# A graph network's edge rounds: matmul operands read in place by a register address, and three transfers a round in place of twelve

## The chip, the cores and the metric

One core of a Trainium2 chip runs the whole kernel in one launch. The time is the device time in microseconds (us) of one execution; the median of three is compared. The engines are TensorE (PE), VectorE (DVE), ScalarE (ACT), GpSimd (POOL) and SyncE (SP). Each runs its own instruction stream, and they are held together by semaphores alone.

## What is computed

The inputs are 6,250 nodes with 256 features and 200,000 edges, sorted by destination. Three layers of graph attention run over the edges and the nodes' own loops; beside them runs a linear-attention mixing block, and behind both a mixture of eight experts. Only the edge part of the attention layers bears on this change:

```python
xh = (h @ W).reshape(n, heads, d)
a_s = (xh * att_src).sum(-1)
a_d = (xh * att_dst).sum(-1)
alpha = jax.nn.leaky_relu(a_s[src] + a_d[dst], NEG_SLOPE)
amax = jax.ops.segment_max(alpha, dst, num_segments=n)
e = jnp.exp(alpha - amax[dst])
z = jax.ops.segment_sum(e, dst, num_segments=n)
alpha = e / (z[dst] + 1e-16)
out = jax.ops.segment_sum(xh[src] * alpha[:, :, None], dst, num_segments=n)
```

The kernel spreads `a_d`, the term of the destination node, over the edges, finds each destination's greatest score, and adds up the weighted rows of the source nodes.

## The kernel before

**Blocks, groups and rounds.** Nodes lie in 49 blocks of 128 (`NB`). Edges are cut into groups of 256 (two halves of 128, one edge per partition), and all edges of a group have their destinations in one block. A round, called a window in the code, takes `WG` = 10 groups, so `WS` = 20 halves; a layer has `NW` = 83 rounds, three layers 249. Buffers of a round come in a ring of `RING` = 4. `over_windows` runs each engine's `step` over the rounds in a loop of four, its first and last rounds written out; each engine has its own order of work for several rounds at once.

**What each engine does in the edge phase.**
- POOL gathers the source nodes' rows, one indirect transfer of 128 rows for each half (L1123). It waits for the indices (L1134 on ScalarE) and, four gathers at a time, for the sums of the round four before, whose buffers it takes.
- SyncE loads per round: four copies of the scan masks and eight small rows of links (`load_masks`, L1026 to L1037), and one broadcast of the edges' place in their block (`load_rels`, 640 KB, L1045). In layer 2 it also loads three constants of the mixing block, behind the first four rounds' masks, and in layer 0 it clears a buffer of the experts.
- ScalarE makes the indices, copies ten node tiles (`load_node`, L1137 to L1143), makes the exponentials of the scores (L1150, L1151) and of the fade (L1160). Its order in a step is: index, exponentials, `load_node` for four rounds ahead, fade, mixing.
- TensorE: `spread_ad` multiplies 20 one-hot halves with the node tiles (L1275), 128 x 12 bf16 for each; `turn` and `turn_back` transpose the scores and the greatest scores (L1284, L1292); `spread_fade` (L1304); `sums` adds the weighted rows of ten groups, four float32 passes each (L1317). Its order in a step is: sums of groups 0 to 4, `spread_fade`, `turn`, sums 5 to 8, `spread_ad` for three rounds ahead, sum 9, the mixing's matmuls, `turn_back`.
- VectorE: one-hots of the edges' places (L1444, L1449), the sums of the spread terms (L1455), scores (L1462, L1467), two scans with the masks over the edges for the greatest score (L1476, L1481), small transposes and scans over the lanes, differences (L1543), weighting of the gathered rows (L1563), one-hots (L1555), and ten adds of the sums into the blocks' accumulators (L1581).

**Block numbers in registers.** Which block each group of a round belongs to is packed in one 32-bit word a round. `blocks_of` (L1014 to L1022) loads the word into a register and unpacks ten block numbers, each from the one before by a shift, a mask and an add. ScalarE and VectorE each run it; ScalarE uses it for the addresses of `load_node`.

**Mixing.** In about the first 49 rounds of each layer a node tile of the mixing block is worked on beside the edges: some 30 more instructions a round on ScalarE, VectorE and SyncE together and about 4 us of matmuls on TensorE (L1329 to L1372), in `mixes`. The rounds behind them have edges only.

**Semaphores that the change touches.** `node_ready` counts ScalarE's filled node tiles, `ad_spread` TensorE's finished spreads, `masks_in[n]` the landed transfers of buffer n, 16 for each of twelve; `walk_out` the transfers of the preparation.

Of the kernel before, what the change touches and what calls it, by code (L numbers as in the profile page):

```python
# [15 lines left out]
BF16 = mybir.dt.bfloat16  # L16
I32 = mybir.dt.int32
ALU = mybir.AluOpType
ACT = mybir.ActivationFunctionType
AX = mybir.AxisListType  # L20

P = 128
# [6 lines left out]
H = 4  # L29
# [5 lines left out]
WG = 10  # L35
WS = 2 * WG
# [82 lines left out]
def prepare_walk(nc, src, dst, st, dr):  # L119
# [6 lines left out]
    with Phase(nc, "walk") as ph:  # L126
# [77 lines left out]
        def _(sp):  # L204
# [34 lines left out]
            for c, n in chunks():  # L239
                sp.dma_start(dr["lanes"].rearrange("(g j) x -> g (j x)", j=2)[c * P:c * P + n, :],  # L240
                             lanes[0:n, c, :, :, :].rearrange("p j m e -> p (j m e)")).then_inc(walk_out, 16)
            sp.wait_ge(links_ready, 2)
# [4 lines left out]
            sp.wait_ge(walk_out, 16 * GC * 6)  # L247
# [564 lines left out]
def edge_phase(nc, layer, st, io, dr):  # L812
# [13 lines left out]
    with Phase(nc, f"edges{layer}") as ph:  # L826
        G = [ph.sb(f"G{r}", [P, WS, GW]) for r in range(RING)]
        index = [ph.sb(f"index{r}", [P, WS], I32) for r in range(RING)]
        node = [ph.sb(f"node{r}", [P, WG, KEPT], BF16) for r in range(RING)]
# [43 lines left out]
        node_ready = ph.sem("node_ready")  # L873
# [151 lines left out]
        def _(sp):  # L1025
            def load_masks(i, n):  # L1026
                w = RING * i + n

                if not isinstance(w, int) or w >= RING:
                    wait_apart(sp, greatest_ready, w - RING + 1, passed_sp)  # L1030
                for h in range(H):
                    sp.dma_start(masks[LANES * h:LANES * h + WS, n, 1:1 + 3 * P], dr["lanes"][bass.ds(w * WS, WS), :]
                                 ).then_inc(masks_in[n], 16)
                for h in range(H):
                    for k, row in ((0, LANES * h), (1, LANES * h + LANES - 1)):
                        sp.dma_start(links[row:row + 1, n, :, :], dr["links"][k:k + 1, :, bass.ds(w * WS, WS)]
                                     ).then_inc(masks_in[n], 16)  # L1037
# [91 lines left out]
        def _(a):  # L1129
# [7 lines left out]
            def load_node(i, n):  # L1137
                w = RING * i + n

                wait_past(a, ad_spread, w - RING + 1)  # L1140
                for g, b in enumerate(blocks_of(a, w)):
                    ins = a.activation(node[n][:, g, :], terms[:, bass.ds(b, 1), :, :].rearrange("p a h k -> p (a h k)"), ACT.Copy)  # L1142
                ins.then_inc(node_ready, 1)  # L1143

# [19 lines left out]
            for n in range(RING):  # L1164
                load_node(0, n)

            def step(i, n, mix):
                if mix:
                    centres(i, n)
                if exists(i, n, 1 + RING):  # L1170
                    make_index(*later(i, n, 1 + RING))
                if exists(i, n, 1):
                    exponentials(*later(i, n, 1))
                if exists(i, n) and exists(i, n, RING):
                    load_node(i + 1, n)
                if exists(i, n, 1):
                    fades(*later(i, n, 1))
                if mix:
                    mixes(i, n)
# [86 lines left out]
        def _(pe):  # L1266
            def spread_ad(i, n):
                w = RING * i + n
                pe.wait_ge(oht_ready, 2 * w + 2)
                pe.wait_ge(node_ready, w + 1)  # L1270

                wait_past(pe, ad_ready, w)
                wait_past(pe, ran, w)
                for s in range(WS):
                    mm = pe.matmul(ps_ad[:, s * KEPT:(s + 1) * KEPT], OHT[:, s, :], node[n][:, s // 2, :], start=True, stop=True)  # L1275
                mm.then_inc(ad_spread, 1)
# [136 lines left out]
        def _(v):  # L1413
# [56 lines left out]
            def scan_on(i, n):  # L1470
                w = RING * i + n
                v.wait_ge(turned, w + 1)
                v.wait_ge(masks_in[n], 16 * 3 * H * i + 16 * 3 * H)
# [1091 lines left out]
def build(nc, io, out):  # L2565

    def dram(name, shape, dt=F32):
# [4 lines left out]
          "lanes": dram("lanes", (2 * NG, 3 * P), BF16), "links": dram("links", (2, 2, 2 * NG), BF16),  # L2572
# [63 lines left out]
```

## Time and profile before

| what | value |
|---|---|
| median of 3 runs | 9471.33 us (9468.83 to 9475.12) |
| profiled execution | 9454.66 us, span 9453.0 us |
| mean granted TensorE clock | 0.724 |
| mean DMA rate over the span | 116 GB/s |
| PE, DVE, POOL, ACT busy | 56%, 58%, 55%, 19% |
| edge phases | three, of 2,449, 2,640 and 2,653 us |

The profile is of one execution. Busy time counts the work of an engine, not its register, branch, semaphore and transfer-issuing instructions. "Idle before" is the time in which the engine did no work ahead of an instruction, and the name behind it what ended that: another engine's instruction, a transfer, "remote" for a semaphore whose raiser the profile doesn't name, or "issue" where the engine waited for nothing that the profile shows, which includes its own register instructions.

### The profile page before, as it was taken

To read this page: it belongs to the slowest core of one execution; us is meant where nothing else is said; L and a number is where in the kernel's file an instruction comes from. 1 tells how busy PE (TensorE), PEld (TensorE's weight loads), DVE (VectorE), ACT (ScalarE), POOL (GpSimd) and SP (SyncE) were. 2 spreads that over 40 slices of the span, in tenths; PEclk is the share of its full clock that TensorE was granted. 3 is DMA by queue.
4 is the path that set the end of the run, shared out by engine and by line. 5 is a ranking of instruction groups with operands and counts; after the bars stand their busy time and mean duration, and the time that the engine had idled before them with its cause. 6 is when DMAs were issued, how large, how long until landed. Compare 5 with 4: busy or idle time off the path is not lost. (4 is left out here: it accounts for less than half of the span.)

```text
span 9453.0 us, 126480 instructions
## 1 busy us (share of the span) xinstructions
PE 5285.4 (56%) x21872; PEld 3724.2 (39%) x21873; DVE 5524.3 (58%) x14694; ACT 1795.1 (19%) x6145; POOL 5206.4 (55%) x5539
## 2 busy tenths in 40 slices
PE   4256666655556255565655556266656565553397
PEld 2144444433334144444443334144444443333255
DVE  4355655555558366665665558366666665557543
ACT  2011111110103012222210002122222220102333
POOL 3566666666662565656566662566666666661332
PEclk7677777776667577777776676577777777766699
DMA  3444444444442343444343333344444443334333
GB/s 118 113 137 130 138 130 136 136 129 133 131 132 87 105 117 111 119 113 118 114 117 110 108 112 108 106 114 121 120 120 120 122 116 112 111 107 132 113 55 75
DMA packets 540784, 1098.15 MB, mean 116 GB/s; under 512 B 136232, under 2 KB 332639, under 8 KB 540147
## 3 DMA queue, kind: packets, MB, share of 16 engines
q0 software_dynamic: 274368, 731.65, 28.9%
q1 hardware_dynamic: 264803, 361.17, 12.1%
q14 instruction: 400, 3.28, 0.1%
q8 instruction: 61, 1.00, 0.0%
q10 hardware_dynamic: 1152, 1.05, 0.0%
HBM read 953.54 MB, written 148.64 MB: 117 GB/s over the span
## 5 line engine op out<-in xcount | busy, mean ns | idle before, releaser
L1123 POOL DMA_INDIRECT edges_G<-rows,edges_index x4980 | 4749.2, 954 | 3076.4 <-issue 1389.8
L1317 PE MATMUL edges_ps_o<-edges_G,edges_OH 128*128 128x264 f32 x9960 | 3620.3, 517 | 2818.6 <-DVE acc L1581 1740.4
L1317 PEld LDWEIGHTS edges_ps_o<-edges_G,edges_OH 128*128 128x128 f32 x9960 | 2357.1, 253 | 3772.9 <-DVE acc L1581 1852.1
L1581 DVE TENSOR_TENSOR acc<-acc,edges_ps_o 128x264 f32 x2490 | 1056.9, 424 | 1992.7 <-remote 1038.9
L1563 DVE TENSOR_TENSOR edges_G<-edges_G,edges_ps_c 128x1024 f32<-128x1024 f32 x1245 | 1501.5, 1206 | 44.1 <-ACT edges_G L1151 33.3
L1142 ACT ACTIVATE edges_node<-terms 128x12 bf16 x2490 | 495.9, 210 | 2316.7 <-issue 2283.7
L1555 DVE TENSOR_TENSOR edges_OH<-edges_ps_c,relT 128x512 f32<-128x512 f32 x1245 | 847.1, 681 | 30.5 <-issue 19.2
L1150 ACT ACTIVATE edges_ps_c<-edges_diff 128x80 f32<-128x80 f32 x249 | 60.0, 241 | 2402.8 <-DVE edges_diff L1543 2174.5
L2400 POOL DMA_INDIRECT x<-experts_Y,experts_token x105 | 162.1, 1544 | 373.5 <-issue 211.5
L1476 DVE TENSOR_TENSOR_SCAN edges_run<-edges_masks,edges_ps_s 128x128 f32<-128x128 bf16 x249 | 102.9, 413 | 444.0 <-ACT edges_fade L1160 286.9
L1275 PEld LDWEIGHTS edges_ps_s<-edges_node,edges_OHT 128*128 128x128 bf16 x4980 | 181.5, 104 | 296.6 <-issue 248.8
L1275 PE MATMUL edges_ps_s<-edges_node,edges_OHT 128*128 128x12 bf16 x4980 | 173.3, 172 | 219.9 <-issue 123.7
L1449 DVE TENSOR_SCALAR edges_OHT<-edges_rels,lane 128x1280 bf16<-128x1280 bf16 x498 | 258.8, 561 | 0.0
L2423 PE MATMUL experts_psH<-W,experts_xs 128*128 x420 | 209.6, 622 | 43.5 <-issue 43.3
L1543 DVE TENSOR_TENSOR edges_diff<-edges_alpha,edges_ps_s 128x80 f32<-128x80 f32 x249 | 57.2, 230 | 301.4 <-DMA xn<-node_Hn 106.3
L799 PE MATMUL node_psB<-node_Wx,node_hT 128*128 128x264 f32 x588 | 213.8, 500 | 0.0
L1988 POOL DMA_INDIRECT xslot<-final_XH,final_slots x98 | 97.6, 996 | 198.0 <-DVE final_slots L2168 169.9
L2438 PE MATMUL experts_psY<-W,experts_hT 128*128 x840 | 198.8, 379 | 0.9 <-DVE experts_hT L2527 0.9
L583 POOL DMA_DIRECT2D rows<-node_ext x147 | 80.0, 544 | 212.1 <-ACT node_ext L757 172.3
L2520 DVE TENSOR_TENSOR experts_hid<-experts_psH,b 128x512 f32<-128x512 f32 x105 | 72.6, 691 | 210.9 <-PE experts_psH L2423 202.9
L1444 DVE TENSOR_SCALAR edges_front<-edges_ps_c,edges_rels 128x128 f32<-128x128 f32 x249 | 85.3, 343 | 133.2 <-DMA edges_rels<-rel 60.1
L1304 PEld LDWEIGHTS edges_ps_s<-edges_dropped,edges_front 128*128 128x128 f32 x498 | 119.7, 241 | 108.8 <-issue 80.7
(345 smaller groups left out, 6399.7 us busy)
## 6 DMA issues: line engine op xcount, KB each, us to landing
edges_rels<-rel SPq DMA_DIRECT2D x249, 640.0 KB
edges_G<-rows,edges_index POOLq DMA_INDIRECT x4980
xslot<-edges_blank SPq DMA_DIRECT2D x80, 650.0 KB
edges_links<-links SPq DMA_DIRECT2D x1992, 0.1 KB
rows<-node_ext POOLq DMA_DIRECT2D x147, 130.0 KB, 2.4
edges_masks<-lanes SPq DMA_DIRECT2D x996, 15.0 KB
experts_X<-xslot SPq DMA_DIRECT2D x105, 130.0 KB, 2.1
node_rows<-rows SPq DMA_DIRECT2D x98, 130.0 KB, 2.1
```

The source lines that it names most:

```text
L799: pe.matmul(psB[slot % 2][:, 0:RW + H], hT[:, slot % TILE_RING, k, :], Wx[:, k, :], start=(k == 0), stop=False)
L1123: g.indirect_dma_start(G[n][:, s, 0:RW], None, dr["rows"], bass.IndirectOffsetOnAxis(index[n][:, s:s + 1], 0)).then_inc(gathered[n], 16)
L1142: ins = a.activation(node[n][:, g, :], terms[:, bass.ds(b, 1), :, :].rearrange("p a h k -> p (a h k)"), ACT.Copy)
L1275: mm = pe.matmul(ps_ad[:, s * KEPT:(s + 1) * KEPT], OHT[:, s, :], node[n][:, s // 2, :], start=True, stop=True)
L1317: mm = pe.matmul(ps_o[BANK_OF[g]][:, 0:GW], OH[:, 2 * g + j, :], G[n][:, 2 * g + j, :], start=(j == 0), stop=(j == 1))
L1449: v.tensor_scalar(OHT[:, s, :].rearrange("p s e -> p (s e)"), rels[:, c * WG * P:(c + 1) * WG * P], lane[:, 0:1], None, ALU.is_equal).then ...
L1555: v.tensor_tensor(OH[:, 4 * k:4 * k + 4, :], ps_iota.unsqueeze(1).broadcast_to([P, 4, P]), rel.unsqueeze(2).broadcast_to([P, 4, P]), ALU.i ...
L1563: v.tensor_tensor(g4[:, :, :, 0:D], g4[:, :, :, 0:D], ps_w[:, 4 * k:4 * k + 4, :].unsqueeze(3).broadcast_to([P, 4, H, D]), ALU.mult).then_ ...
L1581: v.tensor_tensor(a, a, ps_o[BANK_OF[g]][:, 0:GW], ALU.add).then_inc(added, 1)
L2400: g.indirect_dma_start(dr["x2"], bass.IndirectOffsetOnAxis(token[:, slot, :], 0), Y[:, slot, :], None, compute_op=ALU.add).then_inc(y_out, 16)
L2423: mm = pe.matmul(psH[slot % 2][:, :], xs[:, slot % 2, k, :], W1[:, bass.ds(e, 1), k, :].rearrange("p a f -> p (a f)"), start=(k == 0), sto ...
L2438: mm = pe.matmul(psY[slot % 2][:, 0:C], hT[:, slot % 2, c * P:(c + 1) * P], W2[:, bass.ds(e, 1), c, :].rearrange("p a o -> p (a o)"), star ...
```

## The change

Three things change.

1. The node tiles, `load_node` and the semaphore `node_ready` go. TensorE runs `blocks_of` itself at the start of `spread_ad`, and each of the 20 matmuls takes the terms of its block straight from `terms`, at an address that comes from a register.
2. `load_masks` issues 3 transfers a round in place of 12. One fills all 128 partitions of the masks: its source is 32 rows of `lanes`, read four times by a leading dimension of step 0. One transfer fills the first link row of all four heads, one the last. Before, 20 of each 32 partitions were filled, now all 32 (the other 12 get the rows of the groups behind, and no result of them is used).
3. So that the last round's read ends inside `lanes`, that tensor has 12 more rows, and the preparation fills them by one more transfer.

```diff
+            spare = (LANES - WS) // 2
+            sp.dma_start(dr["lanes"].rearrange("(g j) x -> g (j x)", j=2)[NG:NG + spare, :],
+                         lanes[0:spare, 0, :, :, :].rearrange("p j m e -> p (j m e)")).then_inc(walk_out, 16)
...
-            sp.wait_ge(walk_out, 16 * GC * 6)
+            sp.wait_ge(walk_out, 16 * (GC * 6 + 1))
...
-        node = [ph.sb(f"node{r}", [P, WG, KEPT], BF16) for r in range(RING)]
...
-                for h in range(H):
-                    sp.dma_start(masks[LANES * h:LANES * h + WS, n, 1:1 + 3 * P], dr["lanes"][bass.ds(w * WS, WS), :]
+                sp.dma_start(masks[:, n, 1:1 + 3 * P],
+                             dr["lanes"][bass.ds(w * WS, LANES), :].unsqueeze(0).broadcast_to([H, LANES, 3 * P])
+                             ).then_inc(masks_in[n], 16)
+                for k, row in ((0, 0), (1, LANES - 1)):
+                    sp.dma_start(links[row:P:LANES, n, :, :],
+                                 dr["links"][k:k + 1, :, bass.ds(w * WS, WS)].broadcast_to([H, 2, WS])
                                  ).then_inc(masks_in[n], 16)
-                for h in range(H):
-                    for k, row in ((0, LANES * h), (1, LANES * h + LANES - 1)):
-                        sp.dma_start(links[row:row + 1, n, :, :], dr["links"][k:k + 1, :, bass.ds(w * WS, WS)]
-                                     ).then_inc(masks_in[n], 16)
...
-            def load_node(i, n):
-                w = RING * i + n
-
-                wait_past(a, ad_spread, w - RING + 1)
-                for g, b in enumerate(blocks_of(a, w)):
-                    ins = a.activation(node[n][:, g, :], terms[:, bass.ds(b, 1), :, :].rearrange("p a h k -> p (a h k)"), ACT.Copy)
-                ins.then_inc(node_ready, 1)
...
-            for n in range(RING):
-                load_node(0, n)
...
-                if exists(i, n) and exists(i, n, RING):
-                    load_node(i + 1, n)
...
+                blocks = list(blocks_of(pe, w))
                 pe.wait_ge(oht_ready, 2 * w + 2)
-                pe.wait_ge(node_ready, w + 1)
...
-                    mm = pe.matmul(ps_ad[:, s * KEPT:(s + 1) * KEPT], OHT[:, s, :], node[n][:, s // 2, :], start=True, stop=True)
+                    at = terms[:, bass.ds(blocks[s // 2], 1), :, :].rearrange("p a h k -> p (a h k)")
+                    mm = pe.matmul(ps_ad[:, s * KEPT:(s + 1) * KEPT], OHT[:, s, :], at, start=True, stop=True)
...
-                v.wait_ge(masks_in[n], 16 * 3 * H * i + 16 * 3 * H)
+                v.wait_ge(masks_in[n], 16 * 3 * i + 16 * 3)
...
-          "lanes": dram("lanes", (2 * NG, 3 * P), BF16), "links": dram("links", (2, 2, 2 * NG), BF16),
+          "lanes": dram("lanes", (2 * NG + LANES - WS, 3 * P), BF16), "links": dram("links", (2, 2, 2 * NG), BF16),
```

## Rows read from the trace of the kernel before

**Rows 1.** The page's part 1: busy time of each engine.
```profile
PE 5285.4 (56%) x21872; PEld 3724.2 (39%) x21873; DVE 5524.3 (58%) x14694; ACT 1795.1 (19%) x6145; POOL 5206.4 (55%) x5539
```

**Rows 2.** Groups by line (busy us, mean ns | idle us before, by releaser).
```profile
L1123 POOL DMA_INDIRECT edges_G<-rows,edges_index x4980 | 4749.2, 954 | 3076.4 <-issue 1389.8 <-remote 1212.5 <-PE edges_ps_o L1317 439.2
L1317 PE MATMUL edges_ps_o<-edges_G,edges_OH 128*128 128x264 f32 x9960 | 3620.3, 517 | 2818.6 <-DVE acc L1581 1740.4 <-issue 1072.3
...
L1581 DVE TENSOR_TENSOR acc<-acc,edges_ps_o 128x264 f32 x2490 | 1056.9, 424 | 1992.7 <-remote 1038.9 <-issue 698.5 <-PE edges_ps_o L1317 120.9
...
L1142 ACT ACTIVATE edges_node<-terms 128x12 bf16 x2490 | 495.9, 210 | 2316.7 <-issue 2283.7
...
L1476 DVE TENSOR_TENSOR_SCAN edges_run<-edges_masks,edges_ps_s 128x128 f32<-128x128 bf16 x249 | 102.9, 413 | 444.0 <-ACT edges_fade L1160 286.9 <-issue 99.9 <-remote 30.3
```

**Rows 3.** Windows: us; PE, PEld, DVE, ACT, POOL busy; clock; DMA.
```profile
4000.00:5000.00 1000.00, 585.38 (x2510) 428.19 (x2511) 619.44 (x1622) 207.17 (x665) 604.60 (x637) 0.71 0.41 115
...
5689.00:5707.00 18.00, 14.10 (x66) 9.97 (x64) 16.66 (x43) 0.68 (x3) 0.00 (x0) 0.81 0.00 0
```

**Rows 4.** Timeline of POOL in layer 1.
```profile
4504.99 0.95 POOL L1123 DMA_INDIRECT edges_G<-rows,edges_index  x1 [0.30 <-issue]
```

**Rows 5.** Timeline of ScalarE (ACT) in one round of layer 1.
```profile
5002.37 0.46 ACT L1142 ACTIVATE edges_node<-terms 128x12 bf16 x2 [0.39 <-issue]
...
5016.97 0.21 ACT L1142 ACTIVATE edges_node<-terms 128x12 bf16 x1 [3.34 <-issue]
5017.14 0.17 ACT L1160 ACTIVATE edges_fade<-edges_ps_s 128x4 f32<-128x4 f32 x1
```

**Rows 6.** Timeline of ScalarE at layer 1's start.
```profile
3192.43 0.21 ACT L1142 ACTIVATE edges_node<-terms 128x12 bf16 x1 [3.98 <-issue]
```

**Rows 7.** Timeline of VectorE (DVE) at layer 1's start.
```profile
3143.18 0.35 DVE L1444 TENSOR_SCALAR edges_front<-edges_ps_c,edges_rels 128x128 f32<-128x128 f32 x1 [28.58 <-DMA edges_rels<-rel]
...
3195.97 1.22 DVE L1563 TENSOR_TENSOR edges_G<-edges_G,edges_ps_c 128x1024 f32<-128x1024 f32 x1 [16.93 <-ACT edges_G L1151]
```

**Rows 8.** Timeline of VectorE at layer 0's start.
```profile
368.52 1.22 DVE L1563 TENSOR_TENSOR edges_G<-edges_G,edges_ps_c 128x1024 f32<-128x1024 f32 x1 [16.38 <-ACT edges_G L1151]
```

**Rows 9.** Timeline of VectorE at layer 2's start.
```profile
5997.67 0.35 DVE L1444 TENSOR_SCALAR edges_front<-edges_ps_c,edges_rels 128x128 f32<-128x128 f32 x1 [57.91 <-DMA edges_rows<-in_L_mix_ln_b]
```

**Rows 10.** Timeline of SyncE's queue at layer 1's start.
```profile
3126.13 12.34 SPq L1036 DMA_DIRECT2D edges_links<-links  x8
```

**Rows 11.** Lines' register instructions on TensorE (PEldq): ns min/median/max.
```profile
L2371 PEldq FUSED_REGOPS  x330: 42/151/168, 8915.1 to 9419.8; - x165
...
L2371 PEldq TENSOR_LOAD <-owner x210: 296/303/632, 8914.5 to 9419.2; - x105
```

**Rows 12.** The same of one line with a register per matmul operand.
```profile
L2438 PEldq FUSED_REGOPS  x420: 46/46/51, 8922.9 to 9421.0; - x140
```

**Rows 13.** Timeline of TensorE (PE) in a round with mixing.
```profile
4526.50 2.13 PE L1317 MATMUL edges_ps_o<-edges_G,edges_OH 128*128 128x264 f32 x4 [7.96 <-DVE acc L1581]
4528.42 0.73 PE L1275 MATMUL edges_ps_s<-edges_node,edges_OHT 128*128 128x12 bf16 x20
...
4532.73 0.27 PE L1292 MATMUL edges_ps_s<-ident,edges_greatest 128*128 128x128 f32 x1
```

**Rows 14.** Timeline of VectorE in the same round.
```profile
4535.14 0.23 DVE L1543 TENSOR_TENSOR edges_diff<-edges_alpha,edges_ps_s 128x80 f32<-128x80 f32 x1
```

**Rows 15.** Timeline of TensorE in another round with mixing.
```profile
3900.54 0.42 PE L1292 MATMUL edges_ps_s<-ident,edges_greatest 128*128 128x128 f32 x1
```

**Rows 16.** Timeline of VectorE in that round.
```profile
3901.40 0.23 DVE L1543 TENSOR_TENSOR edges_diff<-edges_alpha,edges_ps_s 128x80 f32<-128x80 f32 x1
```

**Rows 17.** Timeline of TensorE in layer 1's last round.
```profile
5696.33 0.47 PE L1292 MATMUL edges_ps_s<-ident,edges_greatest 128*128 128x128 f32 x1 [0.71 <-DVE edges_greatest L1523]
```

**Rows 18.** Timeline of VectorE in that round.
```profile
5699.75 0.23 DVE L1543 TENSOR_TENSOR edges_diff<-edges_alpha,edges_ps_s 128x80 f32<-128x80 f32 x1
```

**Rows 19.** ScalarE's idle time before its fades (us, times).
```profile
  issue: 176.8, 90
```

More of the change, by code:

```diff
@@ L872, in edge_phase @@
         rels_in = ph.sem("rels_in")
-        node_ready = ph.sem("node_ready")
         front_ready = ph.sem("front_ready")
```

## The prediction

> **What bounds the kernel now.** I read the page's busy line first. No engine is above 58% of the span [rows 1], so no engine's work alone sets the end; TensorE (PE), VectorE (DVE) and GpSimd (POOL) wait for one another in a ring. The groups by line say where. Three loops over 249 rounds take some 7,800 of the 9,453 us: POOL's gathers are 4749.2 us busy with 3076.4 us idle before them [rows 2], together 7825.6, or 31.4 us a round. A gather takes 0.954 us, and its neighbours stand 0.30 us apart when nothing holds them [rows 2, 4]: 20 x 1.254 = 25.1 us a round is POOL's floor, and 6.3 us a round are pauses in which POOL waits for sums of the round four back. The other side of the ring, without a gather beside it, runs a round in the 18 us of the second window, DVE busy 16.66 of them [rows 3]. So neither side fills 31.4 us. What stretches the DVE/PE side while POOL gathers is seen in two places: DVE's adds sit idle 1992.7 us, 1038.9 by "remote" and 698.5 by "issue" [rows 2], which is time with nothing that the profile shows to wait for, and PE's sums wait for these adds, 1740.4 us [rows 2].
>
> ScalarE's timeline says what "issue" is. It copies 10 node tiles a round with three register instructions ahead of each. Two copies with 0.39 us before them show the undisturbed rate; some 5 us later in the same round each comes 3.34 us after the last [rows 5], over 1 us for each register instruction. It is so when POOL streams gathers. SyncE's queue shows the same: 8 small transfers take 12.34 us to issue at a layer's start [rows 10]. The copies stand in 495.9 + 2316.7 = 2812.6 us of ScalarE, 11.3 us a round [rows 2]; ScalarE is 19% busy [rows 1], so this costs only where another waits for it.
>
> **The change, part by part.**
> *Layer starts.* Each layer issues 80 gathers at once, and in these 100 us ScalarE makes its first 40 copies and SyncE issues 48 small transfers. The last copy starts at 3192.43 [rows 6], behind it come the next indices and the weights, and DVE has stood 16.93 us for those at 3195.97 [rows 7]; POOL, whose next indices stand behind the same copies, has been idle too. Without the copies I take these 17 us back in layers 0 and 1 each (layer 0 has a wait of 16.38 us [rows 8]). In layer 2, DVE stands 57.91 us for the mixing's row constants, which SyncE issues behind the 48 transfers [rows 9]; 12 transfers take a quarter of the time. Part of that is absorbed, since layer 2's first differences come only 20 us later after its start than layer 1's: 20 us. Sum -54. SyncE's queue also lets the second relT broadcast go earlier (DVE stands 28.58 us for it [rows 7]); but POOL can't pass its 80 gathers, so I give nothing for it here and keep -54 - 3 x 28 = -138 as the other end, and 0 as the near one.
>
> *Fades.* ScalarE's fade stands behind the copies: at 5017.14, right after the last [rows 5]. DVE's scan waits 286.9 us in all for fades [rows 2]. Of the fade's own idle time 176.8 us are issue, in 90 rounds [rows 19]; the rest waits for PE, and with no copies ahead ScalarE will wait for PE instead. So at most 287, at least 0; I take -30, near the low end, because both PE results that the fade needs are late in the same stretches.
>
> *Register instructions beside POOL.* If those of ScalarE, SyncE and DVE share something slow while POOL gathers, then removing some 30 of ScalarE's a round (three per copy) and 9 of SyncE's 12 transfers speeds up DVE's. Bound: DVE's 698.5 us of issue idle at the adds halved, -350, plus the scan's like; the other end 0 (each engine is slow for itself). ScalarE is among its copies for 11.3 of 31.4 us [rows 2], 36%; half of 36% of 698.5 is 126, and I take -100, for SyncE keeps a quarter of its transfers and its relT.
>
> *TensorE reads the terms itself.* The 20 matmuls now take 0.73 us as one block [rows 13]. They get a word load (0.303 us), an address step per group, and a register operand per matmul. The load with what follows takes 0.303 + 0.151 [rows 11]. From below, 19 register instructions and 20 operands at 0.046 each [rows 12] are 1.8 us, 2.2 in all; from above, ScalarE's undisturbed pace of three in 0.39 us [rows 5], 0.13 each, gives 39 x 0.13 + 0.45 = 5.5 us. I take 4.5 (the address steps depend on one another, as ScalarE's do). PE's own register instructions never took more than 168 ns [rows 11]. They begin when the sums before them are issued, and that block runs 2.13 us at 4526.50, so about 2 us are covered; the spread and all behind it in PE's order (the last sums, mixing's matmuls, the turn back) come some 2.5 us later. In rounds without mixing the turn back (5696.33 [rows 17]) runs 3.4 us before DVE comes to the differences (5699.75 [rows 18]), and I cost it at nothing; what hides it is DVE's own queue, and if that cover goes the cost is 2.5 us a round. In the 147 rounds with mixing it is shorter: the turn back at 4532.73 [rows 13], the differences at 4535.14 [rows 14], 2.4 us, and in another round only 0.9, from 3900.54 to 3901.40 [rows 15, 16]. Late by 2.5 us, the two would lose 0.1 and 1.6. Where DVE's adds are what PE waits for (7.96 us at 4526.50 [rows 13]), a late spread is hidden as well. Of a mean of 0.85 I let 0.55 us a round through, 147 x 0.55 = +80. Near end 0; far end, with a push of 3.5 us, losses of 1.1 and 2.6 in the two rounds: 147 x 1.85 = +270. Behind the spread on PE are the last sums, and POOL's release waits for them.
>
> *The transfers.* 3 instead of 12 a round; the masks are loaded four rounds ahead and are used a round or more after they land, so their own landing costs nothing; the cover is a round, 31 us. The broadcast source carries 98 KB instead of 61 KB. In layer 1 the engines are 41% busy moving 115 GB/s [rows 3], 7.2 GB/s each, 17.5 while busy. Spread over 16 engines this adds 2.3 KB each, 0.13 us: nothing. The preparation gets one transfer more, under 1 us in a chain that waits for others.
> The Trainium skill (DMA: Bandwidth & Descriptors, "Why a DMA increments its semaphore by 16" and its rules for authors) says that a leading zero-stride dimension of c copies confines a transfer to at most c engines; here c = 4, where the old shape of 20 partitions gets 10. By it the sum would have a term for four loaded engines, by the rows none is seen; no trace here shows the new shape. It speaks against this change.
>
> **Sum.** -54 - 30 - 100 + 80 = -104. The profiled execution took 9454.66 us (span 9453.0); that is 16.7 below the median of the three runs, 9471.33. So 9350.7 as profiled, 9367 against the median, -1.1%.
>
> **Rivals.**
> 1. *The sum as above*, 9367, its own range 9290 to 9440. Chance 0.40.
> 2. *TensorE's address program is the new wait (slower).* The push is 2.5 to 3.5 us, and in mixing rounds nearly all reaches the differences, then the weights, the next sums, and POOL's release. For it: PE's sums already wait 1740.4 us for DVE, so the ring is tight. Against it: PE is 56% busy and sits idle 2818.6 us at the sums [rows 1, 2]. Price 147 x 1.0 to 1.5 = +150 to +220; with starts -54 and no other relief, 9570 to 9640. It decides once more than 0.4 us of the push in each mixing round reaches the end (147 x 0.4 = 59 against 54). Chance 0.22.
> 3. *Masks on a quarter of the engines (slower).* If the transfer is served by 4 of 16, each gets 24.6 KB, 1.4 us at 17.5 GB/s, 1.2 more than 61 KB over all sixteen. A gather's rows are spread over the engines and land with the slowest, and pauses end some time after the last gather. 249 x 1.2 - 104 = +195: 9666. Against it: each engine is idle 59% of the time [rows 3]. Chance 0.06. It is what the rule of the Trainium skill named above would make of the transfer.
> 4. *POOL's own cadence sets the round.* Run and pause go on as before, the relief on ScalarE is off the path, and the starts' gain pays TensorE's push: -54 + 54, 9471. Chance 0.12.
> 5. *Large relief.* With ScalarE's and most of SyncE's traffic gone, DVE's adds come sooner in every gather run, and the pauses shrink: half of the issue idle (350), half of the fades (143) and the starts (54 to 138) are -547 to -631, and with the push of +80 about 9000; half of it is 9240. Against it: "remote" is more than "issue" before the adds, and waits for PE's results, not for a register. Chance 0.20, its middle 9120.
>
> **How the numbers follow.** 0.2%, 19 us, is what a measurement of this kernel can tell from no change. Faster: 0.40 + 0.20 = 0.60; same 0.12; slower 0.22 + 0.06 = 0.28. The range leaves a tenth at each end: 9150 cuts the large relief in half, and 9590 half of rivals 2 and 3.
>
> **What the profile after would show.** Starts: no idle of 17 us before the first weigh, layer 2's front within 20 us of its start. Fades: the scan's wait for the fade, 286.9, down by 30 or more. Register instructions: the adds' issue idle 698.5 down to about 600. TensorE: the spread's 20 matmuls take 2 to 3 us from first to last instead of 0.73, and the idle before them grows. POOL: idle 3076.4 down by about 100 if I am right, unchanged by rival 4, up by rival 2. What would make me wrong: a register step on PE as slow as on ScalarE during gathers (0.7 us and more), which no PE row shows; then the spread would cost 20 us and the kernel would be far slower.

## The result

| | median, us | runs |
|---|---|---|
| before | 9473.1 | 4 (9468.83 to 9475.12) |
| after | 9551.67 | 4 (9540.29 to 9571.41) |

The ratio is 1.0086, with a 95% interval of 1.0067 to 1.0105: the change made the kernel slower by 0.9%, where faster by 1.1% was forecast. The time lies inside the stated range, and the direction was wrong. The profiled execution has a span of 9558.1 us against 9453.0.

The page's busy line after, which answers to [rows 1]: ScalarE lost 481 us of copies, all others work as before.

```profile
PE 5284.2 (55%) x21872; PEld 3750.7 (39%) x21873; DVE 5519.9 (58%) x14694; ACT 1314.2 (14%) x3654; POOL 5204.1 (54%) x5539
```

The groups by line after (busy us, mean ns | idle us before, by releaser), against [rows 2]. Line numbers have moved: POOL's gathers are L1124, the sums L1307, the adds L1571, the spread L1265, the scan L1466.

```profile
L1124 POOL DMA_INDIRECT edges_G<-rows,edges_index x4980 | 4745.6, 953 | 3184.6 <-issue 1396.7 <-PE edges_ps_o L1307 1038.0 <-remote 714.8
L1307 PE MATMUL edges_ps_o<-edges_G,edges_OH 128*128 128x264 f32 x9960 | 3309.9, 483 | 1735.3 <-DVE acc L1571 1049.2 <-issue 680.8
...
L1571 DVE TENSOR_TENSOR acc<-acc,edges_ps_o 128x264 f32 x2490 | 1055.3, 424 | 2200.9 <-remote 959.0 <-PE edges_ps_o L1307 561.5 <-issue 532.7
...
L1265 PE MATMUL edges_ps_s<-terms,edges_OHT 128*128 x4980 | 465.2, 176 | 1810.4 <-issue 1649.9 <-DVE edges_run L1466 20.9 <-DVE edges_OHT L1439 18.0
...
L1466 DVE TENSOR_TENSOR_SCAN edges_run<-edges_masks,edges_ps_s 128x128 f32<-128x128 bf16 x249 | 102.1, 410 | 168.8 <-ACT edges_fade L1153 92.8 <-DMA node_X<-in_x 23.8 <-issue 20.1
```

Two things that were hoped for are there. The scan waits 168.8 us in place of 444.0, only 92.8 of them for the fade (286.9 before), and the adds' issue idle fell from 698.5 to 532.7. But POOL's idle time rose from 3076.4 to 3184.6, as much as the span grew, and one row stands out: the spread's 20 matmuls sit idle 1810.4 us, 1649.9 of them "issue". Before, their row was this:

```profile
L1275 PE MATMUL edges_ps_s<-edges_node,edges_OHT 128*128 128x12 bf16 x4980 | 173.3, 172 | 219.9 <-issue 123.7 <-DVE edges_run L1476 78.5 <-DVE edges_OHT L1449 17.7
```

Busy and idle together are 2275.6 us, 9.1 us a round against 1.6 before. The adds now wait 561.5 us for TensorE's sums by name (120.9 before), and their idle time as a whole rose, from 1992.7 to 2200.9.

A round of layer 1 with mixing, TensorE's timeline after, beside [rows 13]:

```profile
4550.56 1.16 PE L1307 MATMUL edges_ps_o<-edges_G,edges_OH 128*128 128x264 f32 x4 [0.95 <-DVE acc L1571]
4551.85 1.55 PE L1265 MATMUL edges_ps_s<-terms,edges_OHT 128*128 x10
4555.58 0.22 PE L1265 MATMUL edges_ps_s<-terms,edges_OHT 128*128 x2 [2.18 <-issue]
4559.87 0.20 PE L1265 MATMUL edges_ps_s<-terms,edges_OHT 128*128 x2 [4.07 <-issue]
4563.45 0.22 PE L1265 MATMUL edges_ps_s<-terms,edges_OHT 128*128 x2 [3.38 <-issue]
4565.27 0.54 PE L1265 MATMUL edges_ps_s<-terms,edges_OHT 128*128 x4 [1.60 <-issue]
4565.71 2.12 PE L1307 MATMUL edges_ps_o<-edges_G,edges_OH 128*128 128x264 f32 x4
...
4570.29 0.27 PE L1282 MATMUL edges_ps_s<-ident,edges_greatest 128*128 128x128 f32 x1
```

The spread is no longer one block of 0.73 us. Ten matmuls go by at once, then the rest comes in twos and a four with 1.6 to 4.1 us between, and the spread lasts from 4551.85 to 4565.81, 14 us. The last sums and the turn back (4570.29) stand behind it. The line's own register instructions (ns min/median/max) say why:

```profile
L1265 PEldq ALU_OP  x4731: 3/36/1409, 255.7 to 8653.5; - x198
L1265 PEldq FUSED_REGOPS  x2490: 3/53/1422, 255.8 to 8653.6; - x192
```

The median is 36 and 53 ns, as priced, and single ones take up to 1.4 us. I have counted the register instructions that took over 0.5 us, by engine. Counted are register arithmetic, moves and range checks; loads of a word, branches, waits and the issuing of transfers are left out:

```
kernel                   TensorE  ScalarE  VectorE  SyncE
before                         0     1826      939   1086
after                       1222        0      706    796
```

ScalarE's are gone with its copies; TensorE, which had none, has 1222, 885 us in all. Before, TensorE ran 3,617 register instructions in the edge rounds, 14.5 a round, and none took over 65 ns. After, it runs 11,384 there, 45.7 a round. Of the 1222 long ones 1185 are on the spread's line, in 227 of the 249 rounds; the others are on lines that were there before and were short.

**Where the time went, by place.** From the start of each layer's edge rounds to the first weighting of gathered rows, it took 117.1, 116.2 and 119.5 us before, and 81.9, 92.1 and 108.9 after: 70 us gained. The rest of the edge rounds grew by 58.5, 44.6 and 71.1 us: 174 lost, 104 net. The scans' mean distance says in which rounds (with mixing: from a layer's fifth scan to its 47th; without: from the 55th to the 83rd):

```
us from round to round     layer 0        layer 1        layer 2
with mixing, before/after  31.32 / 31.72  31.77 / 32.51  31.48 / 32.99
without                    30.35 / 30.88  30.34 / 30.38  30.27 / 30.30
```

In layers 1 and 2 the rounds with mixing lose and those without do not; in layer 0 both lose.

VectorE's timeline at the start of layer 1, after, beside [rows 7], with TensorE's turn back (L1282) ahead of it; and of layer 2, beside [rows 9]:

```profile
3159.14 0.45 PE L1282 MATMUL edges_ps_s<-ident,edges_greatest 128*128 128x128 f32 x1
...
3193.37 0.24 DVE L1533 TENSOR_TENSOR edges_diff<-edges_alpha,edges_ps_s 128x80 f32<-128x80 f32 x1 [53.70 <-DMA h<-node_Hn]
...
3194.60 1.21 DVE L1553 TENSOR_TENSOR edges_G<-edges_G,edges_ps_c 128x1024 f32<-128x1024 f32 x1
```

```profile
5997.25 0.35 DVE L1434 TENSOR_SCALAR edges_front<-edges_ps_c,edges_rels 128x128 f32<-128x128 f32 x1 [11.89 <-DMA edges_b<-in_L_mix_b]
```

The 16.93 us wait for ScalarE's weights is gone, and layer 2's wait for its constants is 11.89 us in place of 57.91. The differences at 3193.37 come 53.70 us after VectorE's last work. Some 20 us of that are the turn back: it stands behind a spread that lasts from 3136.71 to 3159.29, full of register instructions of 0.7 us. The other 33.8 us lie between the turn back's end and the differences, which by the code wait for nothing else in a layer's first round; the transfer that the row names is of the part before. The kernel before has the same gap, 29.8 us. It is no register instruction, and what makes it isn't shown.

### The profile page after: what moved, and what is told of

It is laid out like the page before. It is cut to its first block and busy times, and to the rows that moved or that the text cites. A ratio compares the mean times of both kernels' runs of the same rounds, so it can differ in the third digit from the quotient of the medians.

```text
span 9558.1 us, 119805 instructions
## 1 busy us (share of the span) xinstructions
PE 5284.2 (55%) x21872; PEld 3750.7 (39%) x21873; DVE 5519.9 (58%) x14694; ACT 1314.2 (14%) x3654; POOL 5204.1 (54%) x5539
## 5 line engine op out<-in xcount | busy, mean ns | idle before, releaser
L1124 POOL DMA_INDIRECT edges_G<-rows,edges_index x4980 | 4745.6, 953 | 3184.6 <-issue 1396.7
L1307 PE MATMUL edges_ps_o<-edges_G,edges_OH 128*128 128x264 f32 x9960 | 3309.9, 483 | 1735.3 <-DVE acc L1571 1049.2
L1307 PEld LDWEIGHTS edges_ps_o<-edges_G,edges_OH 128*128 128x128 f32 x9960 | 2197.8, 236 | 2521.4 <-DVE acc L1571 1158.6
L1571 DVE TENSOR_TENSOR acc<-acc,edges_ps_o 128x264 f32 x2490 | 1055.3, 424 | 2200.9 <-remote 959.0
L1265 PE MATMUL edges_ps_s<-terms,edges_OHT 128*128 x4980 | 465.2, 176 | 1810.4 <-issue 1649.9
L1265 PEld LDWEIGHTS edges_ps_s<-terms,edges_OHT 128*128 128x128 bf16 x4980 | 309.5, 106 | 2050.3 <-issue 2033.3
L1153 ACT ACTIVATE edges_fade<-edges_ps_s 128x4 f32<-128x4 f32 x249 | 43.1, 173 | 1953.7 <-PE edges_ps_s L1274 535.9
L1978 POOL DMA_INDIRECT xslot<-final_XH,final_slots x98 | 98.8, 1009 | 196.8 <-DVE final_slots L2158 168.8
L1466 DVE TENSOR_TENSOR_SCAN edges_run<-edges_masks,edges_ps_s 128x128 f32<-128x128 bf16 x249 | 102.1, 410 | 168.8 <-ACT edges_fade L1153 92.8
L2428 PEld LDWEIGHTS experts_psY<-W,experts_hT 128*128 128x128 f32 x840 | 151.8, 191 | 17.9 <-issue 1.6
```

The lines of the kernel that those rows point to most:

```text
L1124: g.indirect_dma_start(G[n][:, s, 0:RW], None, dr["rows"], bass.IndirectOffsetOnAxis(index[n][:, s:s + 1], 0)).then_inc(gathered[n], 16)
L1307: mm = pe.matmul(ps_o[BANK_OF[g]][:, 0:GW], OH[:, 2 * g + j, :], G[n][:, 2 * g + j, :], start=(j == 0), stop=(j == 1))
L1571: v.tensor_tensor(a, a, ps_o[BANK_OF[g]][:, 0:GW], ALU.add).then_inc(added, 1)
L2428: mm = pe.matmul(psY[slot % 2][:, 0:C], hT[:, slot % 2, c * P:(c + 1) * P], W2[:, bass.ds(e, 1), c, :].rearrange("p a o -> p (a o)"), star ...
```

## The experiments

All ratios are to runs of the kernel before on the same chip, taken with them. The kernel before takes 9473 us on the first chip, 9382 us on the one of the first four experiments (A, number 9 in the record), and 7854 to 7858 us on those of all the others (B, numbers 3, 12, 8 and 3 again). Runs of one kernel on one chip agree to 0.5%, those of the kernel before to 0.3%. Each chip was met once or twice, so whether the difference belongs to the chip or to something else at that time isn't shown; "chip" stands for both below. Ratios are formed only within a chip. The full change itself was measured on the first chip and on one of B, never on A.

### The two parts apart (chip A)

Transfers alone: 3 a round in place of 12, ScalarE's copies as before.

```diff
-                for h in range(H):
-                    sp.dma_start(masks[LANES * h:LANES * h + WS, n, 1:1 + 3 * P], dr["lanes"][bass.ds(w * WS, WS), :]
+                sp.dma_start(masks[:, n, 1:1 + 3 * P],
+                             dr["lanes"][bass.ds(w * WS, LANES), :].unsqueeze(0).broadcast_to([H, LANES, 3 * P])
...
```

> The transfers' part of the change alone: 3 transfers a round, node copies on ScalarE as before. Theory S (an engine has a stock of instructions that it can run while POOL streams gathers; past it each costs about 0.7 us; the loss comes from TensorE's 29 new register instructions a round): this kernel has none of them and is faster than before, by the starts' share (layer 2's row constants come early, about 20 us) and some relief, 9420 to 9455 us. Rival M (the masks transfer on few transfer engines lengthens the gathers): slower by 100 us or more, 9570 or above, and POOL's idle time grows as in the full change (3076 to 3185).

Measured: ratio 0.9865 (0.9849 to 0.9882), 9255.26 us. The expectations of these four gave times for the first chip. As a ratio this one was 0.994 to 0.998, so the gain is larger than was expected. TensorE has no register instruction over 0.5 us, ScalarE 1838.

```profile
L1126 POOL DMA_INDIRECT edges_G<-rows,edges_index x4980 | 4750.0, 954 | 2884.9 <-issue 1373.1 <-remote 969.8 <-PE edges_ps_o L1320 507.3
...
L1278 PE MATMUL edges_ps_s<-edges_node,edges_OHT 128*128 128x12 bf16 x4980 | 173.8, 173 | 134.7 <-DVE edges_run L1479 61.7 <-issue 37.7 <-DVE edges_OHT L1452 35.3
```

Terms alone: 12 transfers, TensorE reads the terms by registers.

```diff
-                    load_node(i + 1, n)
...
+                blocks = list(blocks_of(pe, w))
...
-                pe.wait_ge(node_ready, w + 1)
...
+                    at = terms[:, bass.ds(blocks[s // 2], 1), :, :].rearrange("p a h k -> p (a h k)")
...
```

> The node terms' part alone: TensorE reads them by a register, ScalarE copies nothing, 12 transfers a round as before. Theory S: the loss is all here; the starts' gain from ScalarE (17 us in layers 0 and 1) stays, so 9560 to 9600 us, and TensorE's register instructions of the spread show some 1200 that take over 0.5 us. Rival M: no loss here, 9400 to 9450.

Measured: ratio 1.0305 (1.0282 to 1.0328), 9660.1 us, where 1.009 to 1.013 was expected; 1391 register instructions of TensorE over 0.5 us.

```profile
L1121 POOL DMA_INDIRECT edges_G<-rows,edges_index x4980 | 4758.3, 955 | 3269.5 <-issue 1388.4 <-PE edges_ps_o L1304 1268.5 <-remote 577.6
...
L1262 PE MATMUL edges_ps_s<-terms,edges_OHT 128*128 x4980 | 475.5, 176 | 2158.2 <-issue 1997.8 <-DVE edges_OHT L1436 35.7 <-DVE edges_run L1463 4.2
```

What follows: the loss is all in the terms' part, +278 us, and the transfers' part by itself is worth -127 us, far more than the 20 us I gave it. POOL's idle time follows: 2884.9 against 3269.5. That the masks' transfer lengthens the gathers (rival 3) is out: a gather takes 954 ns as before. The two ratios multiply to 1.017, where the full change had 1.0086 on the first chip; whether the parts help each other or the chips differ isn't shown. Nor is the transfers' gain in the starts. With the transfers alone it takes 115.7, 115.2 and 115.8 us from a layer's first gather to its first weighting, and with the kernel before, on the first chip, 116.4, 115.5 and 118.8, although layer 2's wait for its constants is down to 11.5 us here too.

### Take away TensorE's registers, or move them (chip A)

The full change with a fixed address. The spread takes the terms of blocks 0 to 9, which are those of other nodes; all else is computed.

```diff
-                blocks = list(blocks_of(pe, w))
...
-                    at = terms[:, bass.ds(blocks[s // 2], 1), :, :].rearrange("p a h k -> p (a h k)")
+                    at = terms[:, s // 2:s // 2 + 1, :, :].rearrange("p a h k -> p (a h k)")
```

> The full change, but the 20 matmuls of a round read the terms of blocks 0 to 9, a fixed address, so TensorE has no register instructions for them (the spread terms are then those of other nodes; all else is computed as before). Theory S: nothing is late on TensorE, ScalarE and SyncE are relieved, the starts gain 70 us: 9330 to 9400 us. If the register instructions are not the cause (rival M, or matmuls reading from the large tensor), it stays near 9550.

Measured: ratio 0.9786 (0.977 to 0.9803), 9181.28 us, better than the 0.985 to 0.992 expected, and no long register instruction on TensorE or ScalarE.

```profile
L1124 POOL DMA_INDIRECT edges_G<-rows,edges_index x4980 | 4764.7, 957 | 2785.9 <-issue 1373.3 <-remote 989.5 <-PE edges_ps_o L1306 388.3
...
L1264 PE MATMUL edges_ps_s<-terms,edges_OHT 128*128 128x12 bf16 x4980 | 171.3, 172 | 98.8 <-issue 51.7 <-DVE edges_OHT L1438 39.2 <-DVE edges_run L1465 7.9
```

The spread's idle time is 98.8 us. This kernel has all of the change but the registers: the same matmuls on the same large tensor, no copies, three transfers. Its matmuls take 172 ns each, as with the copies, and it is faster than the transfers alone (0.9865). So reading in place from the large tensor costs nothing that shows, and what costs in the terms' part is TensorE's register work, which includes the word's load. The ratio is also close to the rest of the prediction's sum: -54 - 30 - 100 = -184 us is -1.9%, and -2.1% was measured.

The full change, with the unpacking spread over TensorE's step, one block number ahead of each group's sums:

```diff
+                coming = blocks_of(pe, RING * i + n + 3) if exists(i, n, 3) else iter(())
                 if here:
-                    sums(i, n, range(0, 5))
+                    for g in range(0, 5):
+                        found += [b for b in [next(coming, None)] if b is not None]
+                        sums(i, n, range(g, g + 1))
...
```

> The full change, with TensorE's unpacking of the ten block numbers spread over its step: one ahead of each group's sums, where TensorE mostly waits for VectorE's adds anyway; the same instructions in number. Theory S: the stock runs out as before, since it counts all instructions, but part of the cost falls into waits: 9480 to 9550 us. Rival B (only a burst of register instructions is slow, spaced ones are not): 9340 to 9420 and no register instruction of TensorE over 0.5 us.

Measured: ratio 0.993 (0.9913 to 0.9947), 9308.24 us. TensorE still has 1055 register instructions over 0.5 us, so rival B, that only a burst is long, falls. Busy and idle of the spread are 1717 us in place of 2276 on the first chip. The ratio is below the range that I gave for theory S (1.001 to 1.008), and inside the one for rival B (0.986 to 0.994); it is the count of long instructions that decides against B, not the time. That TensorE's waits for VectorE cover more of the cost than I had thought is my reading, not shown.

```profile
L1124 POOL DMA_INDIRECT edges_G<-rows,edges_index x4980 | 4745.2, 953 | 2937.0 <-issue 1373.2 <-remote 849.1 <-PE edges_ps_o L1306 680.0
...
L1264 PE MATMUL edges_ps_s<-terms,edges_OHT 128*128 x4980 | 373.4, 175 | 1343.6 <-issue 1216.1 <-DVE edges_OHT L1445 35.1 <-DVE edges_run L1472 20.9
```

### Chips on which nothing is late (chips B)

Chip A has no trace of the kernel before, so the next three had one beside them.

> The kernel before, unchanged, for a profile from the chip on which the next three run. Both theories: 9350 to 9480 us, as the chip has it.

Measured: 7856.21 us, against 7854.13 for the runs around it. The expectation was off by 1,500 us. Groups by line of this unchanged kernel on this chip, beside [rows 2]:

```profile
L1123 POOL DMA_INDIRECT edges_G<-rows,edges_index x4980 | 4730.0, 950 | 1550.4 <-issue 1477.7 <-ACT edges_index L1134 38.9 <-PE edges_ps_o L1317 33.8
...
L1581 DVE TENSOR_TENSOR acc<-acc,edges_ps_o 128x264 f32 x2490 | 1052.9, 423 | 244.0 <-DVE acc L1581 136.1 <-PE edges_ps_o L1317 35.0 <-issue 14.9
...
L1142 ACT ACTIVATE edges_node<-terms 128x12 bf16 x2490 | 486.8, 209 | 119.0 <-issue 58.4
```

POOL's gathers take 950 ns as before (954). But their idle time is 1550.4 us, 0.31 us each: POOL pauses nowhere within a layer. Rounds come every 25.1 us, which is the floor of 20 x 1.254 us that the prediction worked out. The adds sit idle 244.0 us in place of 1992.7, with neither "remote" nor "issue" as the main releaser, and ScalarE's ten copies run at the pace that I called undisturbed. At a layer's start the differences follow the turn back at once. Not one register instruction of any engine takes over 0.5 us. The transfer engines were busy 34.9% of this span with the gathers' queue and 28.9% of the longer one, 2741 and 2732 us: the packets themselves are no faster.

The three that ran with it put instructions back on SyncE, put them back on ScalarE, or moved ScalarE's fade ahead of the copies:

```diff
+                    at = nc.s_assert_within(sp.snap(at + (list(blocks_of(sp, w))[-1] >> 6)), 0, WS * (NW - 1), skip_runtime_bounds_check_because=ROWS_SEEN)
```

> The transfers' part alone (3 transfers a round), and SyncE gets 28 register instructions a round in the loops, ahead of the masks' transfer: it loads the word, unpacks all ten block numbers and adds a zero made of the last to the address. The transfers alone were faster than before by 1.35%. Theory S with one supply shared by the engines: the gain came from fewer instructions on SyncE, so it goes, ratio 0.995 to 1.01. Rival T (the gain is that of the transfers themselves, 9 small ones fewer on the transfer engines): the ratio stays at 0.985 to 0.99.

```diff
+            def registers(i, n):
+                b = list(blocks_of(a, RING * i + n))[-1]
+                a.activation(scratch[:, :], terms[:, bass.ds(b, 1), 0, 0:1].rearrange("p a k -> p (a k)"), ACT.Copy)
```

> The fixed-address kernel (the spread reads the terms of blocks 0 to 9), with one thing put back: ScalarE unpacks the ten block numbers where the copies stood and uses the last for one copy of 128x1; 31 instructions a round, nine copies fewer than before. The fixed address alone had ratio 0.979. Theory S, shared: ScalarE's instructions run past its stock again, some 1500 take over 0.5 us, they slow VectorE's, ratio 0.985 to 0.995. Rival (each engine has its own supply, and ScalarE is off the path but for fades): 0.978 to 0.984.

```diff
-                if exists(i, n) and exists(i, n, RING):
-                    load_node(i + 1, n)
                 if exists(i, n, 1):
                     fades(*later(i, n, 1))
+                if exists(i, n) and exists(i, n, RING):
+                    load_node(i + 1, n)
```

> The transfers' part alone, and in ScalarE's step the fade now stands ahead of the ten node copies. If the fade behind the copies costs what the profile shows (the scan waits some 185 us for it in the transfers-only kernel), 50 to 150 us come off 0.9865: ratio 0.972 to 0.981. If the fade is late because TensorE's results are seen late, nothing: 0.985 to 0.990; slower than 0.990 if the copies then hold up the next index.

Measured: 0.9996, 0.9997 and 0.9997, each within 0.001. On such a chip they tell nothing of each other. The changed kernel was then measured there as well:

> The changed kernel, unchanged, beside the next three. On the chip of the last call the kernel before took 7854 us, its gathers stood 25.1 us a round and no register instruction took over 0.5 us; on a chip like that all versions are bound by POOL's gathers and this one has ratio 0.999 to 1.001. On a chip like the first two (9471 and 9382 us) it has 1.005 to 1.015.

Measured: 1.0001 (0.9992 to 1.0011), 7855.24 us. TensorE's timeline in a round with mixing shows what the spread costs when no register instruction is long:

```profile
3501.22 1.16 PE L1307 MATMUL edges_ps_o<-edges_G,edges_OH 128*128 128x264 f32 x4 [1.94 <-DVE acc L1571]
3502.37 0.20 PE L1265 MATMUL edges_ps_s<-terms,edges_OHT 128*128 x2
3502.74 1.19 PE L1265 MATMUL edges_ps_s<-terms,edges_OHT 128*128 x8 [0.17 <-issue]
3504.08 1.19 PE L1265 MATMUL edges_ps_s<-terms,edges_OHT 128*128 x8
3505.42 0.22 PE L1265 MATMUL edges_ps_s<-terms,edges_OHT 128*128 x2 [0.15 <-issue]
3505.54 2.12 PE L1307 MATMUL edges_ps_o<-edges_G,edges_OH 128*128 128x264 f32 x4
```

From the end of the sums ahead of it to the start of the last sums it is 3.2 us, for the word's load (3501.32 to 3501.62) runs beside the sums ahead. The unpacking instructions (ns min/median/max) stay within 41 ns, and POOL's row is that of the kernel before:

```profile
L1265 PEldq ALU_OP  x4731: 32/36/41, 255.5 to 6955.8; - x198
```

```profile
L1124 POOL DMA_INDIRECT edges_G<-rows,edges_index x4980 | 4729.1, 950 | 1550.6 <-issue 1468.8 <-ACT edges_index L1135 41.0 <-PE edges_ps_o L1307 40.8
```

The same three kernels were measured three times more, each time on a chip B (7854.2, 7857.75 and 7853.6 us for the kernel before). SyncE's registers:

> The transfers' part alone (3 a round) and 28 register instructions a round on SyncE, as before, since the last chip couldn't tell. On a chip on which the kernel before takes some 9400 us: one shared supply of instructions, 0.995 to 1.01; the gain is that of the transfers, 0.985 to 0.99. On one with 7854 us: 1.000 either way.

> The transfers' part alone and 28 register instructions a round on SyncE. Chips with 7854 us for the kernel before (two so far) leave this open. On one with some 9400 us: a supply of instructions that the engines share, 0.995 to 1.01; a gain that is the transfers' own, 0.985 to 0.99.

> The transfers' part alone and 28 register instructions a round on SyncE; three chips with some 7855 us leave it open. On one with some 9400 us: a shared supply of instructions, 0.995 to 1.01; the transfers' own gain, 0.985 to 0.99. On one with 7855 us: 1.000.

Measured: 0.9996, 0.9999, 0.9997. ScalarE's registers:

> The fixed-address kernel with ScalarE's unpacking put back, as before. On a chip of 9400 us: shared supply, 0.985 to 0.995; own supplies, 0.978 to 0.984. On one of 7854 us: 1.000.

> The fixed-address kernel with ScalarE's unpacking put back. On a chip with some 9400 us: shared supply, 0.985 to 0.995; own supplies, 0.978 to 0.984. On one with 7854 us: 1.000.

> The fixed-address kernel with ScalarE's unpacking put back. On a chip with some 9400 us: shared supply, 0.985 to 0.995; own supplies, 0.978 to 0.984. On one with 7855 us: 1.000.

Measured: 0.9996, 0.9996, 0.9999. The fade ahead of the copies:

> The transfers' part alone with the fade ahead of the copies. On a chip of 9400 us: 0.972 to 0.981 if the copies make the fade late, 0.985 to 0.990 if TensorE's results are seen late. On one of 7854 us: 1.000.

> The transfers' part alone with the fade ahead of the copies. On a chip with some 9400 us: 0.972 to 0.981 if the copies make the fade late, 0.985 to 0.990 if TensorE's results are seen late. On one with 7854 us: 1.000.

> The transfers' part alone with the fade ahead of the copies. On a chip with some 9400 us: 0.972 to 0.981 if the copies make the fade late, 0.985 to 0.990 if TensorE's results are seen late. On one with 7855 us: 1.000.

Measured: 0.9995, 0.9997, 1.0001. All are 1.000, as expected for such a chip, and the questions behind them stay open.

## Why the prediction was wrong

**The step that failed** is in the costing of TensorE's reading: "PE's own register instructions never took more than 168 ns [rows 11]", and with it the 4.5 us for the spread, a push of 2.5 us and the term of +80. The sentence is true of TensorE as it was. The rows shown for it are of the experts' part, after 8915 us, but it holds in the edge rounds too: 3,617 register instructions there, none over 65 ns. What failed is to carry it over to an engine that runs three times as many of them beside the gathers. On a chip where nothing is long the push is as I costed it: the spread takes 3.2 us in the mean from its first matmul's start to its last one's end, 2.6 more than with the copies. (I had counted 39 instructions at 0.05 to 0.13 us; there are 29 between the matmuls.) On the first chip it takes 8.7 us in the mean and 14 in the round shown, because 1222 of TensorE's 11,384 took over 0.5 us. I had named slow steps as what would make me wrong, and gave them no chance of their own; I also took them to come all or none (20 us a spread, far slower), where one in nine came. The rows that spoke for it were ScalarE's [rows 5], an engine with 35.7 register instructions a round in the same stretch, 1826 of them over 0.5 us.

**Rival 2 has the place and the price, with too small a push.** It priced the loss at 150 to 220 us, and 174 were measured behind the starts, net of all relief there. It laid the loss in the rounds with mixing, +0.40, +0.74 and +1.51 us a round; next to nothing is lost in those without in layers 1 and 2, but +0.53 a round in layer 0. It took a push of 2.5 to 3.5 us; the mean push is 7.5 us (9.1 less 1.6), so a smaller share of the push reached the end than it assumed. The differences' wait for TensorE's turn back is its trace, 127.0 us in this row of the waits (total, times, longest), where it was 15.1 in 12 times:

```profile
DVE edges_diff L1533 <- PE edges_ps_s L1282: 127.0, 59, 4.8
```

**The other terms.** Starts: 54 forecast (17, 17, 20), 70 measured (35, 24, 11). Adds' issue idle: about 600 forecast, 532.7 measured; how much of it became time is not shown. Fades: the scan's wait fell by 194 us where I gave 30 us of time; how much of it became time is not shown. TensorE: +80 forecast; the terms' part alone costs +278 us on chip A with its gains already in it, and the register instructions, between the fixed address there (0.9786) and the full change on the first chip (1.0086), some 3%, an estimate across two chips. Transfers: costed at nothing beyond the starts and an unnamed part of the -100, measured at -127 us on chip A. Rival 3 and the rule of the Trainium skill behind it (DMA: Bandwidth & Descriptors, "Why a DMA increments its semaphore by 16") bore on the one thing that made no loss: the transfers' part alone is faster on chip A, and the kernels that contain it are equal to the kernel before on chips B. On how many engines it ran no row here shows.

**What stays open.** Why nine fewer small transfers are worth 1.35% on chip A. They take with them the instructions that issue them; whether those or the transfers are what counts, the kernels made for it couldn't tell on chips B. Why TensorE's register instructions become long is open as well. Two readings of the traces bear on it.

First, do the engines share one supply? VectorE has fewer long ones when ScalarE runs no copies: 939 and 950 with the copies (before, transfers alone), 688 to 769 in the four kernels without them. But with none on TensorE (fixed address) it has 769, and with 1391 there (terms alone) it has 688, and SyncE's number goes with its own transfers: 1086 and 1084 with twelve a round, 768 to 835 with three, whatever ScalarE and TensorE do. So one supply for all engines isn't borne out; the counts are from two chips.

Second, how likely a register instruction is long depends on how many instructions its engine has run since 4 us after POOL began a stretch of gathers (a pause over 0.6 us ends one; for TensorE its weight loads count). On SyncE, before, it is 40% of the first five and 86% of the next five; on VectorE up to 6% up to the twentieth and 60% from the thirtieth; on TensorE after the change 5% of the first thirty and 45% from the fortieth. It looks like a stock that each engine brings along and then an entry every 0.7 us, which is the median of the long ones on each engine. That is a guess. Against a plain count stands the kernel before: 104 of TensorE's register instructions came behind its thirtieth there, and none was long. And why some chips have this and others not, no run here tells.

**A version that beats both** is the transfers' part alone: 0.9865 on chip A, and on chips B the kernels that contain it, with more instructions or another order besides, are within 0.001 of the kernel before. On the first chip it was not run.

## What to carry to other kernels

A price that an engine shows for a few instructions need not hold when it is given three times as many. Even the right engine in the right stretch (3,617 short ones) would have misled here; the warning was on the engines that ran many beside the gathers, ScalarE above all. Moving register work to an engine that shows none of the trouble can bring the trouble along, and that engine's order decides what it holds up: here it stood ahead of the last sums and of the turn back. And whether two versions differ by a few per cent can depend on the chip: on one where GpSimd's gathers are the bound, 20 x 1.254 us a round, all of these versions are the same.

## What the runs showed that I had not expected

The same program takes 9473, 9382 and 7854 us on different chips, each steady to 0.3%, with the same duration of the gathers (954 and 950 ns), of the adds (424 and 423 ns) and of the transfers' packets. Three things differ in the traces. There are register instructions of up to 1.7 us beside gathers, on ScalarE, VectorE and SyncE, and after the change on TensorE. VectorE goes on late after TensorE's results: at layer 1's start the differences begin 29.8 us after the turn back that they wait for, and 0.0 us after it on chip B; before the adds, "remote" ends 1038.9 us of idle time, and is not among the main releasers at 7856 us. And TensorE's mean granted clock is 0.724 against 0.784, with 517 and 479 ns for a matmul of the sums. Which of these is cause and which effect isn't shown. Nearly the whole difference of 1,600 us is in the edge rounds, 31.0 against 25.1 us each, 249 times, and in their starts, 351 against 157 us.
